# Two-layer attention and gated-unit stack: query and key pieces regrouped by half heads, the swapped projection dropped

## The reference, cut to what matters

```
h = shift_token(x);  q, k, v = split(h @ wqkv)           # each (8 heads x 64)
q = l2norm(q) * qs;  k = l2norm(k) * ksc                  # norm over the 64 of a head
q = q*cos*scale + rotate_half(q)*sin*scale                # rotate_half: (x1, x2) -> (-x2, x1)
k = k*cos/scale + rotate_half(k)*sin/scale
o = softmax(8 * q k^T over own and previous window, masked) @ v
x = x + o @ wo
h = layernorm(shift_token(x)) ;  a, g = split(h @ w1 + b1) ;  x = x + (a * gelu(g)) @ w2 + b2
```

## Time and profile before

| what | value |
|---|---|
| median of three runs | 2607.54 us |
| profiled execution | 2607.92 us, of which the span is 2606.1 us |
| mean granted PE clock | 0.91 of full speed |
| busy: PE, DVE, ACT, POOL | 2062.2, 1543.1, 1350.0, 878.5 us |
| ffn0, ffn1 | about 31 to 563 us and 1055 to 1588 us of the span |
| a row of ffn0 from one L800 to the next | 62.16 us (rows 1, 2), 60.13 us (rows 3 to 6), 46.13 us (row 7) |

### The profile page before, as it was taken

The page is one execution under the profiler, slowest core; times in us unless marked ns, Lnnn a source line. Parts: engine busy times, 40 slices in busy tenths (PEclk is TensorE's granted clock), DMA queues, the critical chain, the costliest instruction groups (busy, mean ns, idle before and its releaser), DMA issues. The chain is left out here.

```text
span 2606.1 us, 40905 instructions
## 1 busy us (share of the span) xinstructions
PE 2062.2 (79%) x13536; PEld 1270.8 (49%) x13536; DVE 1543.1 (59%) x2523; ACT 1350.0 (52%) x2990; POOL 878.5 (34%) x660
## 2 busy tenths in 40 slices
PE   3788988976988986688898985497688878885596
PEld 2455555532555554355555552386244644542385
DVE  5566565546799797465566655486344344335486
ACT  3566666636799796466666665142522222224242
POOL 1322323225677676132223321433133032002432
PEclk9899999986799799699999997698799999896698
DMA  6000000011000001000000002201200000000202
GB/s 238 1 1 1 1 1 1 1 53 56 18 25 19 23 19 45 0 1 1 1 1 1 1 1 102 68 23 50 97 0 0 0 0 0 0 0 8 67 22 65
DMA packets 44351, 66.31 MB, mean 25 GB/s; under 512 B 7552, under 2 KB 33536, under 8 KB 42784
## 3 DMA queue, kind: packets, MB, share of 16 engines
q1 hardware_dynamic: 39664, 55.11, 6.7%
q0 software_dynamic: 4544, 9.35, 1.1%
HBM read 48.40 MB, written 21.18 MB: 27 GB/s over the span
## 5 line engine op out<-in xcount | busy, mean ns | idle before, releaser
L1465 POOL TENSOR_TENSOR arena<-arena 128x1024 f32<-128x1024 f32 x128 | 299.7, 2362 | 131.7 <-ACT arena L1399 131.7
L944 POOL TENSOR_TENSOR arena<-arena 128x512 f32<-128x512 f32 x128 | 132.9, 1039 | 497.1 <-DVE arena L789 494.8
L319 PE MATMUL PS<-arena_r 128*128 128x512 f32 x408 | 204.0, 500 | 89.4 <-DVE arena_r L1886 43.6
L938 POOL TENSOR_TENSOR arena<-arena 128x512 f32<-128x512 f32 x128 | 164.6, 1286 | 214.1 <-DVE arena L757 175.7
L629 ACT ACTIVATE arena<-PS,arena 128x128 f32<-128x128 f32 x512 | 179.9, 366 | 56.3 <-DVE arena L782 55.6
L1373 PE MATMUL PS<-con,arena 128*128 128x128 f32 x1024 | 157.2, 298 | 48.4 <-DVE arena L1449 46.0
L768 DVE SCALAR_TENSOR_TENSOR arena<-arena 128x512 f32<-128x512 f32 x128 | 88.6, 692 | 156.9 <-POOL arena L938 124.1
L1449 DVE COPY arena<-PS 128x512 f32<-128x512 f32 x256 | 165.7, 684 | 21.3 <-PE PS L1373 21.2
L1373 PEld LDWEIGHTS PS<-con,arena 128*128 128x128 f32 x1024 | 118.8, 150 | 121.4 <-issue 94.6
L1399 ACT ACTIVATE arena<-PS,arena 128x512 f32<-128x512 f32 x256 | 154.9, 688 | 43.8 <-DVE arena L1430 42.3
L1410 ACT ACTIVATE arena<-arena 128x512 f32<-128x512 f32 x256 | 162.5, 636 | 23.4 <-DVE arena L1437 17.3
(11 more groups left out here) (363 smaller groups left out, 4994.1 us busy)
## 6 DMA issues: line engine op xcount, KB each, us to landing
big<-in_gu SPq DMA_DIRECT2D x16, 512.0 KB, 7.8
sorted_x<-in_slots SPq DMA_DIRECT2D x2, 2515.5 KB, 15.3
arena<-sorted_x SPq DMA_DIRECT2D x6, 774.0 KB, 7.2
big<-in_dn SPq DMA_DIRECT2D x16, 256.0 KB, 8.2
arena<-expert_y SPq DMA_DIRECT2D x16, 256.0 KB, 3.4
big<-in_wqkv SPq DMA_DIRECT2D x2, 1536.0 KB, 8.3
arena<-q_split SPq DMA_DIRECT2D x96, 32.0 KB
arena<-k_split SPq DMA_DIRECT2D x96, 32.0 KB
```

What stands on the lines that cost most here:

```text
L319: pe.matmul(bank, w_hi, hi, start=first, stop=False)
L938: g.tensor_tensor(t_rot[:, j % 2, :], t_cos[:, j % 2, :], t_sin[:, j % 2, :], ALU.add).then_inc(s("qk_rotated"), 1)
L944: g.tensor_tensor(pn[:, u % 2, :, :], pr[:, u % 2, :, :], pinv[:, u % 2, :].unsqueeze(2).broadcast_to([P, TPB, P]), ALU.mult).then_inc(s(" ...
L1465: g.tensor_tensor(a, a, mk[:, hp, 2 * half:2 * half + 2, :], ALU.mult).then_inc(s("a_masked"), 1)
```

## The change

A piece is now one half (32 channels) of each of four heads: piece 0 of a pair holds the first halves, piece 1 the second halves of the same heads. A pair has both halves on the same partitions of two PSUM banks, so the rotation is made from two pieces, and `wswap` goes, with its load, its splits and its products. There are four pairs for eight pieces; per pair DVE makes four multiplications and two scalings, ACT two squares, POOL three additions (the squares, and the two rotated halves), PE one sum. The learned scales enter as a column of the multiplications and no longer by scaling the tables at load. Scores contract over 32 partitions and add both halves: 32 matmuls for a pair of heads. On DVE `hidden` stands ahead of `entered`. The hand-written order of the tail is rewritten for four pairs.

```diff
-            def piece_bank(r, j):          # and PIECES = 8 -> PAIRS = 4
+            def pair_bank(r, j):
 def project(r, j):
-                w = tuple(a[:, layer, c * P:(c + 1) * P] for a in (wqkv_hi, wqkv_lo))
-                product(pe, PS[:, o, :], w, *h).then_inc(s("proj"), 1)
-                w = tuple(a[:, layer, 2 * c:2 * c + 2, :, :].rearrange("p a b c -> p (a b c)") for a in (wswap_hi, wswap_lo))
-                product(pe, PS[:, o + 1, :], w, *h).then_inc(s("proj"), 1)
+                for half in range(2):
+                    c = slice(first + half * P, first + half * P + P)
+                    product(pe, PS[:, o + half, :], tuple(a[:, layer, c] for a in (wqkv_hi, wqkv_lo)), *h).then_inc(s("proj"), 1)
 def sums(r, j):
+                pe.wait_ge(s("sq_summed"), START + J + 1)
+                pe.matmul(PS[:, pair_bank(r, j) + 2, :], blk32, t_sum[:, j % 2, :], start=True, stop=True).then_inc(s("qk_sums"), 1)
 def scores(r, c):
-                if c == 0:
-                    pe.wait_ge(s("qk_scaled"), START + at(N, PIECES, PIECES))
+                if c % 2 == 0:
+                    pe.wait_ge(s("qk_scaled"), START + at(N, 2 * PAIRS, PAIRS if r and c == 0 else 2 * PAIRS))
...
+                    for half in range(2):
+                        i = c // 2 * 2 + half
+                        for w in range(2):
+                            a = t * P + w * WINDOW
+                            for par in range(2):
+                                h = HALF * (2 * (c % 2) + par)
+                                h = slice(h, h + HALF)
+                                mm = pe.matmul(PS[w * WINDOW:(w + 1) * WINDOW, par, t * P:(t + 1) * P], qs[h, i, a:a + WINDOW],
+                                               ks[h, i, a:a + 2 * WINDOW], start=False, stop=half == 1, skip_group_check=True)
 def squares(r, j):
+                for half in (1, 0):
+                    if half:
+                        act.wait_ge(s("proj"), START + at(N, 2 * PAIRS, 2 * j + 2))
+                    else:
+                        act.wait_ge(s("rot_products"), START + at(N, 4 * PAIRS, 4 * j + 2))
+                    act.activation(t_sq[:, j % 2, half, :], PS[:, pair_bank(r, j) + half, :], ACT.Square).then_inc(s("qk_squared"), 1)
 def rotate(r, j):
+                for half in range(2):
+                    v.wait_ge(s("proj"), START + at(N, 2 * PAIRS, 2 * j + half + 1))
+                    if half:
+                        v.wait_ge(s("qk_squared"), START + at(N, 2 * PAIRS, 2 * j + 1))
+                    for i in range(2):
+                        v.scalar_tensor_tensor(t_prod[:, j % 2, 2 * half + i, :], PS[:, pair_bank(r, j) + half, :],
+                                               fcol[:, layer, kind + half:kind + half + 1], rot[:, kind + (i + half) % 2, :],
+                                               ALU.mult, ALU.mult).then_inc(s("rot_products"), 1)
 def row(r) on DVE:
+                if p is not None:
+                    hidden(p)
                 if nx is not None:
                     entered(nx)
-                if p is not None:
-                    hidden(p)
 def rotated(r, j) on POOL:
+                g.wait_ge(s("qk_squared"), START + 2 * J + 2)
+                g.tensor_tensor(t_sum[:, j % 2, :], t_sq[:, j % 2, 0, :], t_sq[:, j % 2, 1, :], ALU.add).then_inc(s("sq_summed"), 1)
+                g.tensor_tensor(t_rot[:, j % 2, 0, :], t_prod[:, j % 2, 0, :], t_prod[:, j % 2, 2, :], ALU.subtract).then_inc(s("qk_rotated"), 1)
+                g.tensor_tensor(t_rot[:, j % 2, 1, :], t_prod[:, j % 2, 1, :], t_prod[:, j % 2, 3, :], ALU.add).then_inc(s("qk_rotated"), 1)
...
-            v.wait_ge(s("rot_scaled"), START + 8)
```

More of the change, by code:

```diff
@@ L32 @@
 INNER = HEADS * DH
+HALF = DH // 2
+GROUP = P // HALF
 QK_SCALE = 8.0
@@ L111, in rotary_tables @@
     sc = base[None].astype(np.float64) ** power[:, None].astype(np.float64)
[L112 to L116, removed]
+    cos, sin, sc = np.cos(fr).T, np.sin(fr).T, sc.T
+    tabs = [cos * sc * QK_SCALE, sin * sc * QK_SCALE, cos / sc, sin / sc]
+    return np.stack([np.tile(a, (GROUP, 1)) for a in tabs], 1).astype(np.float32)
 def position_tables():
@@ L720, in ffn_act @@
             entered(0)
-            for w, hi, _ in weights[2:]:
+            for w, hi, _ in weights[1:]:
                 act.activation(hi, w, ACT.Copy).then_inc(s("weights_high"), 1)
-            for j in range(PIECES + 1):
-                if j < PIECES:
+            for j in range(PAIRS + 1):
+                if j < PAIRS:
                     squares(0, j)
@@ L771, in take_values @@
+                for half in range(2):
+                    v.wait_ge(s("qk_rotated"), START + 2 * J + half + 1)
+                    dst = ks[:, 2 * c + half, WINDOW:] if j % 2 else qs[:, 2 * c + half, :]
+                    v.scalar_tensor_tensor(dst, t_rn[:, j % 2, :], 1e12, t_rot[:, j % 2, half, :], ALU.min,
+                                           ALU.mult).then_inc(s("qk_scaled"), 1)
             def take_values(r, i):
@@ L945, in normalised @@
                                 pinv[:, u % 2, :].unsqueeze(2).broadcast_to([P, TPB, P]), ALU.mult).then_inc(s("p_normed"), 1)
-            for j in range(PIECES):
+            for j in range(PAIRS):
                 rotated(0, j)
@@ L952, in ffn_pool @@
                 rotated(r + 1, 0)
+                normalised(r, 6)
                 rotated(r + 1, 1)
-                normalised(r, 6)
+                normalised(r, 7)
                 rotated(r + 1, 2)
-                normalised(r, 7)
-                for j in range(3, PIECES):
-                    rotated(r + 1, j)
+                rotated(r + 1, 3)
         def ffn_zero_pads(g, f):
@@ L2645, in _layouts @@
     fc = np.zeros((P, DEPTH, 16), wqkv.dtype)
-    vecs = [two(qs), two(swap(qs)), two(ks), two(swap(ks)), g["L0_ffn_ln_g"], g["L0_ffn_ln_b"], g["L0_ffn_b2"]]
+    vecs = [four(a[..., i:i + HALF]) for a in (qs, ks) for i in (0, HALF)] + [g["L0_ffn_ln_g"], g["L0_ffn_ln_b"], g["L0_ffn_b2"]]
     vecs += [b1a[:, c] for c in range(3)] + [b1g[:, c] for c in range(3)]
```

204 lines of the change are left out of this document (78 added, 126 removed).

## The result

The changed kernel takes 2670.23 us (median of four runs, 2656.84 to 2683.16); before, run beside it, 2607.31 us. The ratio is 1.024, with a 95% interval of 1.018 to 1.030: slower, by some 60 us. The prediction was 2682, range 2612 to 2708. The spread of the changed kernel's runs is 1%, where the kernel before has 0.25%; runs with a lower mean granted clock are the longer ones (0.875 in that of 2656.84 us, 0.863 in that of 2683.16). The profiled execution took 2665.16 us, 57.2 us more than that of before.

What follows compares the result with a forecast made beforehand. PE was taken to bound a row's first half, a serial chain across DVE, ACT, POOL and PE its tail. 2607.9 + 14.8 (rows and starts) + 63 (lost clock) - 3.4 (wait before L503 gone) = 2682 us, range 2612 to 2708.

Steps and rivals of the forecast that it cites:

- First half of a row: Row up to the tail: PE bounds; score passes +1.03 us each, `hidden` ahead of `entered` removes the wait before L503.
- the rival on the scores: Score passes: both halves run side by side in the array, no pass costs more; about 17 us per stage, 2648; chance 0.10.
- The halves of a score: Score passes: 32 matmuls take twice the time of 16, +1.03 us a pass, not overlapping fully.
- The chain of a pair: Tail: multiplications, squares, POOL's addition, sum, norm, scalings run serially; a pair recurs every 7.5 us against 2 x 3.35 = 6.7.
- The whole tail: From the start of `proj(0)` through the last pair: 33.05 us where it was 32.15, +0.9 us.
- The clock: Tails: sparse PE work drops it to 1.2 GHz in every tail; 4.5 us each, 14 x 4.5 = 63 us.
- the case that came: Tails: the clock recovers in between, so about 2.5 us per tail remain instead of 4.5.
- The start of a stage: Before the first scores: chain of 4.7 us a pair, scores at 67.0 instead of 76.42; taken as -8.5 us per stage.
- scaling 1.22: Start of a stage, on DVE: the two scalings of a pair, 0.61 us each, within its 4.7 us.
- The rival "PE bounds the tail": Tail: PE is the bound, so saved products and sums shorten each by 8 us; about 2498; chance 0.12.
- Its deciding point: Tail: PE-bound tails decide the outcome once a pair recurs in less than 6.3 us.
- 14.8 - 3.4: Both stages: +14.8 us for rows and starts at full clock; -3.4 for the vanished wait before L503 in ffn1.

Runs made afterwards that it cites:

- e10: e9's later gaps filled and the second half of every score left out (doesn't compute the layer); 2601.06 us, ratio 0.996.
- e9: Changed kernel with two unused 128x512 matmuls on TensorE ahead of the second, third and fourth sum of each tail; 2630.12 us, ratio 1.007.
- e2: Changed kernel with the two squared halves summed on TensorE by two accumulating matmuls instead of GpSimd's addition; 2566.36 us, ratio 0.981.
- e6: Changed kernel with both e5's mended order and e2's squares summed on TensorE; 2584.66 us, ratio 0.990.
- e3: Changed kernel with the tail one pair behind: next pair's projection and multiplications ahead of this pair's sum and scalings; 2673.97 us, ratio 1.022.
- e5: e3 with the last sum ahead of the last products with the values, and the last two transposed copies ahead of scalings; 2627.74 us, ratio 1.007.
- e8: Changed kernel with the split of the next row's input ahead of the gated units again; 2678.41 us, ratio 1.028.

## Why the prediction was right

Sign, mechanism and size held: 2682 forecast, 2670 measured. Step by step:

- **First half of a row.** Forecast +0.5 us to `proj(0)` in rows 1 and 2, +1.0 in rows 3 to 6. Measured from the row's start: 30.13 against 30.01 us in row 2, 28.79 against 28.00 in row 4, so +0.1 and +0.8. Right as a net. A pass costs 0.87 us more, not 1.03. The net hides two parts whose size only the runs show: 29 us for the doubled scores (e10 beside e9; the rival on the scores had 34), and a gain for the gated units, 15 us in the kernel before.
- **The halves of a score.** They don't run side by side: 32 matmuls take 1.91 us, 16 took 1.04, and their removal gives 29 us. The rule on contractions of 32 by which they would be free (the Trainium skill, TensorEngine Tiling, Theoretical Speedup) does not come to bear in this loop, which names two groups of partitions in a pass. Whether that is the reason is not shown; a loop over four groups was not tried.
- **The chain of a pair.** Forecast 7.5 us at the full clock. With the clock held, in the tail of row 4 of e9, sums and scalings are 7.3 to 7.9 us apart; in that of the changed kernel, with the clock lost, 8.2 to 8.9. The whole tail was to take 33.05 us at the full clock; the twelve tails of e9's windows take 33.2 in the mean. Right. PE idle 3 to 4 us ahead of L410: measured 2.9 to 3.9.
- **The clock.** Lost in every tail, as forecast, down to 0.89 in the rows. The term was mis-sized: 63 us forecast (4.5 us a tail), about 40 by e9 (2.8 a tail). The prediction had named the case that came, that the clock recovers between the sums (2.5 us a tail), and set it aside. L476 was to take 5 to 6 us and took 4.08, since the clock came back during it; the whole tail of row 4 is 36.1 us (360.92 to 397.02) for 32.15, which is +3.95 instead of +5.4. What the prediction cites on the throttled state stands in the Trainium skill (TensorE: Matmul & The Clock Gate) one section further on, under What's actually happening.
- **The start of a stage.** Forecast scores at 67.0, measured 70.19. The step that failed is "scaling 1.22" for a pair: with GpSimd adding beside them two scalings take 2.96 to 3.42. The loop before has one addition per piece, which never overlaps with a scaling (DVE waits for it; all 128 of L768 took 0.69 us), so the rows before could not show it. It costs 3 us of the 8.5 in a stage.
- **The rival "PE bounds the tail".** Refuted by PE's own row: PE is idle 152.5 us ahead of L410 alone. Its deciding point (a pair in under 6.3 us) is a fair one, though: e2 comes to 5.9 to 6.8 and is faster than before.

The forecast was 12 us too long, and two errors offset each other in it. By the ratios the clock cost 45 us where 63 were forecast, and all the rest 17 us (e9) where 11 were (14.8 - 3.4); the two starts, 3 us short each, are as much as that difference of 6. So the closeness of 2682 to 2670 is in part luck, and the interval of the changed kernel's ratio (about 15 us to each side) is wider than what is left to explain.

## What to carry to other kernels

Before judging a saving on the busiest engine, write down the chain of one step of the loop and its order on every engine; an addition that joins two halves costs its length wherever the chain waits for it, and here two accumulating matmuls beat one addition on GpSimd by 104 us. A gap in TensorE's work costs its own length and then the clock of what follows; useful work in the gap, or a link less in the chain, returns both. Before overlapping two engines' work, find out which pairs slow each other, and what the new order puts at the end of the tail: both speak against e6.

## What the runs showed of the hardware

- **VectorE beside GpSimd.** A scaling (two inputs from SBUF, 128x512 f32) takes 0.69 us alone and up to 1.75 beside GpSimd's additions. They take turns: at 56.75 us of the changed kernel's trace GpSimd's addition starts first and takes its usual 1.26; the scaling that starts at 56.81 ends only at 58.56; the addition behind it takes 1.71; both scalings together take 3.42 (1.29 alone). The multiplications, whose first input is PSUM, take 0.67 us each beside the same additions (six in 4.04 us from 45.81 us of the start of ffn0). The Trainium skill (SBUF — State Buffer, SBUF: two separate sides) has the pair of ports that both engines need as a lock that the other waits for, for VectorE's operations with two SBUF inputs; the trace agrees, with 3.42 us for two scalings beside GpSimd's additions.
- **The clock falls in sparse work, not only in idle stretches.** In the row shown PE works for 52.5 of 64.9 us and has the full clock in the first half; in the tail, with gaps of 2.9 to 3.9 us between bursts, L410 runs at 1.2 GHz (2.08 us) again and again. With gaps of up to 2.07 us (e9) or 1.58 us (e2) it ran at the full clock in the tails shown. One gap alone doesn't decide it: in the two starts of a stage L410 follows a wait of 3.02 us both times, and takes 2.08 us in ffn0 and 1.12 in ffn1.
- **The spread of runs.** The changed kernel's four runs spread by 1%, the four of before beside them by 0.25%. That is not tied to the clock that falls: e9, with the clock held, spreads by 1% over ten runs, e3, with 0.93 in its rows, by 0.2% over four, and the fourteen runs of before beside e5 to e8 by 0.7%.
